# A graph network's count matrices on one core: layer-norm statistics ahead of all tiles, early turnings inside row 0, later rows placed in halves

## The reference, cut to what matters

```python
h = relu(layernorm(x))
# L0: three edge convolutions, all on the same edges
#   s[n] = sum over edges e with dst[e]=n of  concat(h[n], h[src[e]] - h[n]) @ W_l + b_l
#   h_l  = relu(s / max(cnt, 1));   cat = [h, h_1, h_2, h_3];   x1 = x + cat @ Wf + bf
# L1: one weighted convolution
#   agg[n] = sum over edges of edge_weight[e] * (relu(layernorm(x1)) @ W)[src[e]]
#   out = x1 + relu(batchnorm(agg + bias))
```

## Time and profile before

| | |
|---|---|
| median of 3 runs | 120.38 us |
| the three runs | 120.27, 120.38, 121.62 us |
| the profiled execution's own time | 121.34 us |
| its span (first to last instruction) | 118.6 us |
| mean granted TensorE clock | 0.992 |
| PE busy | 105.4 us (89%) |
| DVE busy | 96.0 us (81%) |
| ACT busy | 61.3 us (52%) |
| POOL busy | 26.9 us (23%) |

### The profile page before, as it was taken

One profiled execution on the slowest core, in us unless ns is written; L12 is line 12 of the kernel. 1 busy time (PEld: TensorE's weight loads), 2 busy tenths in 40 slices (PEclk: granted clock), 3 DMA queues, 4 the chain that ended last, 5 costly groups with the idle time before them and its releaser, 6 DMA issues.

```text
span 118.6 us, 2664 instructions
## 1 busy us (share of the span) xinstructions
PE 105.4 (89%) x1023; PEld 97.8 (82%) x1023; DVE 96.0 (81%) x269; ACT 61.3 (52%) x143; POOL 26.9 (23%) x32
## 2 busy tenths in 40 slices
PE   0298999999999999999989999999899998999740
PEld 0146889898799998998889999999899988998530
DVE  2499999999997999599997489965999979607970
ACT  2597765999679999330270613531613153223530
POOL 7100000000000069926039650099100000000000
PEclk9999999999999999999999999999999999999996
DMA  2967700000030000000050200000000000000025
GB/s 45 238 177 204 247 21 0 0 0 6 3 88 6 0 6 6 3 8 0 0 177 14 80 0 0 0 6 0 0 0 6 0 0 0 3 0 0 0 63 153
DMA packets 5400, 4.62 MB, mean 39 GB/s; under 512 B 555, under 2 KB 5386, under 8 KB 5386
## 3 DMA queue, kind: packets, MB, share of 16 engines
q1 hardware_dynamic: 4460, 3.68, 10.5%
q10 hardware_dynamic: 926, 0.75, 2.5%
HBM read 3.79 MB, written 0.64 MB: 37 GB/s over the span
## 4 chain that ended last, share of the span: by engine, by line
PE 60%; DVE 22%; POOL 6%; issue 4%; DMA 3%; ACT 3%; SPq 0%; DVEq 0%; POOLq 0%
PE bank L1217 11%; PE bank L1068 9%; PE bank L1312 9%; PE bank L1070 9%; PE bank L1069 9%; DVE src_hot L568 5%; PE bank L1130 4%; PE bank L1141 4%; DMA edge_rows_i<-in_dst_dram 3%; POOL parts L462 3%; POOL parts L464 2%; DVE stats L518 2%; PE bank L1108 2%; PE bank L1352 2%; DVE pre L732 2%
## 5 line engine op out<-in xcount | busy, mean ns | idle before, releaser
L1217 PEld LDWEIGHTS bank<-dst_hot,src_hot 125*128 125x128 bf16 x505 | 25.6, 104 | 3.5 <-DVE src_hot L568 1.8
L1217 PE MATMUL bank<-dst_hot,src_hot 125*128 125x112 bf16 (+6 forms) x505 | 27.7, 215 | 0.8 <-DVE src_hot L568 0.2
L568 DVE TENSOR_SCALAR src_hot<-node_id,edge_cols 125x626 bf16<-125x626 f16 x77 | 24.1, 380 | 0.6 <-PE bank L1217 0.6
L462 POOL TENSOR_TENSOR parts<-parts 125x625 f32<-125x625 f32 x5 | 7.0, 1391 | 46.4 <-DVE raw L575 39.2
L1312 PE MATMUL bank<-counts,u_lo 125*128 125x312 f32 (+1 forms) x60 | 16.3, 308 | 0.0
L1012 ACT ACTIVATE h_hi<-pre 128x312 fp32r<-128x312 f32 (+1 forms) x12 | 5.6, 468 | 18.0 <-DVE pre L732 18.0
L1312 PE MATMUL bank<-counts,u_hi 125*128 125x312 f32 (+1 forms) x48 | 14.0, 307 | 0.0
L879 ACT ACTIVATE parts<-bank 125x375 f32<-125x375 f32 x25 | 13.0, 536 | 0.0
L1312 PEld LDWEIGHTS bank<-counts,u_lo 125*128 125x128 f32 x60 | 10.9, 189 | 0.0
L1312 PEld LDWEIGHTS bank<-counts,u_hi 125*128 125x128 f32 x48 | 9.1, 189 | 0.0
L879 ACT ACTIVATE counts<-bank 125x125 fp32r<-125x125 f32 (+1 forms) x25 | 7.9, 317 | 1.1 <-PE bank L1217 1.1
(11 more groups left out here) (137 smaller groups left out, 258.6 us busy)
## 6 DMA issues: line engine op xcount, KB each, us to landing
raw<-in_L_gnn_W_dram SPq DMA_DIRECT2D x3, 512.0 KB, 6.8
x_in<-in_x_dram ACTq DMA_DIRECT2D x1, 560.0 KB
raw<-in_L_gnn_Wf_dram SPq DMA_DIRECT2D x1, 512.0 KB, 3.8
wf<-in_L_gnn_Wf_dram SPq DMA_DIRECT2D x1, 256.0 KB, 7.9
raw<-in_L_gnn_Wf_dram SPq DMA_DIRECT2D x1, 256.0 KB, 2.7
raw<-in_L_gnn_W_dram SPq DMA_DIRECT2D x1, 256.0 KB, 4.8
out_dram<-x_in SPq DMA_DIRECT2D x1, 224.0 KB
out_dram<-x_in SPq DMA_DIRECT2D x1, 168.0 KB
```

The lines of the kernel that those rows point to most:

```text
L462: step.add(pool.tensor_tensor(part[:, :, 1, :], part[:, :, 1, :], part[:, :, 2, :], ALU.add))
L568: dve.tensor_scalar(src_hot[:, t % RING, 0:IDS], node_id[:, 0:IDS], edge_cols[:, 0, t:t + 1], None, ALU.is_equal).then_inc(src_hot_vector, 1)
L1217: return pe.matmul(built[s][:, :, n0:n0 + n], src_hot[:, t % RING, BLK * s:BLK * s + P], dst_hot[:, c, :, j // 2, c0:c0 + n, j % 2], start ...
```

## The change: what it does

The statistics of x are all taken at once, ahead of the first weighted window, and the scale and shift right behind that window, before DVE's first tile. ACT makes tiles 0 and 4 early, then root, h0 and its copies, then tiles 22 and 27 with the high half of u's blocks 0 and 1 between them, and only then row 0's copies. PE runs ten matmuls without use instead of four, turns h0's blocks ahead of row 0's pieces 2, 4, 6, 9 and 9, the vectors ahead of piece 5, and makes u's blocks 0 and 1 ahead of piece 8. The banks of all these groups are named: the vectors have bank 6, and h0's block 3 is the next group in it. DVE reads the vectors at t = 18, u's low halves at t = 24, 37, 41. Rows 3 and 4 are placed in two halves as well.

```diff
-SCALAR_EARLY, SCALAR_LATER = (0, 4, 9), {0: (36, 40), 1: (55,), 2: (72, 76)}
-SCALAR_TILES = SCALAR_EARLY + sum(SCALAR_LATER.values(), ())
-STATS_AT, SHIFT_AT, VECS_AT, DIFF_AT = (1, 2, 3, 5, 6), 8, 19, 37
-U_AT = (34, 39, 42)
-DEV_AT, FLAG_AT = 40, 74
+SCALAR_EARLY, SCALAR_NEXT, SCALAR_LATER = (0, 4), (22, 27), {0: (36, 40), 1: (55,), 2: (72, 76)}
+SCALAR_TILES = SCALAR_EARLY + SCALAR_NEXT + sum(SCALAR_LATER.values(), ())
+VECS_AT, DIFF_AT = 18, 33
+U_AT = (24, 37, 41)
+DEV_AT, FLAG_AT = 43, 74
@@ the banks
-        groups.plan([("h0", b) for b in range(2)], h0_t_ready, 1)
-        groups.plan(["vecs"], vecs_ready, 1)
-        groups.plan([("h0", b) for b in range(2, NB)], h0_t_ready, 3)
-        for blocks in U0_BLOCKS:
-            groups.plan([("u", 0, blocks[0])], u_lo_ready, blocks[-1] + 1)
-        groups.plan([("own", 0, q) for q in range(4)], own_ready, 1)
-        groups.plan(["dev"], flag_ready, 1)
+        groups.plan([("h0", b) for b in range(2)], h0_t_ready, 1, banks=(7, 5))
+        groups.plan(["vecs"], vecs_ready, 1, banks=(6,))
+        groups.plan([("h0", 2)], h0_t_ready, 3, banks=(7,))
+        groups.plan([("u", 0, 0)], u_lo_ready, 2, banks=(5,))
+        groups.plan([("h0", b) for b in range(3, NB)], h0_t_ready, 4, banks=(6, 7))
+        groups.plan([("u", 0, 2)], u_lo_ready, 4, banks=(6,))
+        groups.plan([("u", 0, 4)], u_lo_ready, 5, banks=(7,))
+        groups.plan([("own", 0, q) for q in range(4)], own_ready, 1, banks=(5, 6, 7, 5))
+        groups.plan(["dev"], flag_ready, 1, banks=(6,))
@@ DVE
+            dve.wait_ge(x_loaded, 32)
+            for b in range(NB):
+                moments_of(b)
+            variances(range(NB))
             weighted_window(0)
+            scale_shift(range(NB), norm_ready)
             dve.wait_ge(edge_cols_ready, 1)
             for t in range(TILES):
-                if t in STATS_AT:
-                    dve.wait_ge(x_loaded, 32)
-                    moments_of(STATS_AT.index(t))
-                if t == STATS_AT[-1] + 1:
-                    variances(range(NB))
-                if t == SHIFT_AT:
-                    scale_shift(range(NB), norm_ready)
                 if t == VECS_AT:
@@ ACT
-            for t in SCALAR_EARLY[:3]:
+            for t in SCALAR_EARLY:
                 source_tile(t)
...
             root(rstd[0:BLK, 0:NB], moments[0:BLK, 0:NB, 1])
-            for t in SCALAR_EARLY[3:]:
-                source_tile(t)
...
             h0_high(NB - 1)
+            for t in SCALAR_NEXT:
+                source_tile(t)
+                if t == SCALAR_NEXT[0]:
+                    high_rows(("u", 0, 0), 0, 2)
...
                     copy_block(r, s)
-                    if r == 0 and s in (1, 3, 4):
-                        blocks = U0_BLOCKS[s // 2]
-                        high_rows(("u", 0, blocks[0]), blocks[0], len(blocks))
+                    if r == 0 and s == 2:
+                        high_rows(("u", 0, 2), 2, 2)
+                    if r == 0 and s == 4:
+                        high_rows(("u", 0, 4), 4)
@@ PE
-            keep_warm(4)
+            keep_warm(10)
...
-            jobs = {9: (0,), 11: (1,), 12: (2,), 14: (3,), 15: (4,)}
+            jobs = {2: (0,), 4: (1,), 6: (2,), 9: (3, 4)}
...
-                chunks = ((0, n // 2), (n // 2, n)) if r in (1, 2) else ((0, n),)
+                chunks = ((0, n // 2), (n // 2, n))
...
-                        if i == 12:
+                        if i == 5:
                             turn_vecs()
+                        if i == 8:
+                            neighbour_terms_0(U0_BLOCKS[:1])
                         for b in jobs.get(i, ()):
                             turn_h0(b)
...
-                            if r == NB - 1 and s == NB - 1:
+                            if r == NB - 1 and s == NB - 1 and chunk[0] == 0:
                                 sum_counts(1, fill(("cnt", 1))).then_inc(filled, 1)
...
                 if r == 0:
-                    neighbour_terms_0()
+                    neighbour_terms_0(U0_BLOCKS[1:])
```

More of the change, by code:

```diff
@@ L1120, in feature_rows, with neighbour_terms_0 @@
                 return [(hi[:, k, BLK * b:BLK * (b + 1)], lo[:, k, BLK * b:BLK * (b + 1)]) for k in range(KF)]
-            def neighbour_terms_0():
+            def neighbour_terms_0(groups_of_blocks):
                 pe.wait_ge(raw_loaded[0], 16)
-                for blocks in U0_BLOCKS:
+                for blocks in groups_of_blocks:
                     o = fill(("u", 0, blocks[0]))
```

## The result

The changed kernel takes 123.7 us (median of four, 123.6 to 124.62) against 120.57 (120.27 to 121.62): ratio 1.0306, 95% interval 1.025 to 1.0363. That is 3.1 us slower, where 0.8 was forecast, and above the top of the range, 122.7. The span of the profiled execution grew from 118.6 to 121.8 us.

The account below looks back on a forecast made before the run. The end was taken to hang on when DVE finishes tile 84: +1.73 wait for u, -0.29 for a tile, -0.64 wait at tile 68 gave +0.80 us, 121.2 us carried to the median; range 119.4 to 122.7.

Parts of the forecast that it names:

- The named banks cost nothing else.: Bank plan: u's banks 6 and 7 and own's banks are free in time, so no further cost.
- the last of the signs of being wrong: Layer 1, near 60 us: the forecast is wrong if PE and not DVE's head chain releases it.
- rival 2: PE's row 0: the clock stays low through it, by turnings or the new gap; +3.0 us, 123.4 us, chance 0.08.
- The vectors' wait: PE in front of piece 9 of row 0: a new wait of about 1.0 us, until 16.4, for DVE's copy.
- DVE's wait for u: DVE at t = 24: waits 1.73 us, 17.86 to 19.6, for the high half of u from ACT.
- DVE's finish: DVE's end of tile 84, at difference(1): 41.94 + 1.73 - 0.29 - 0.64 = 42.74, +0.80 us.
- The statistics: DVE ahead of all tiles: moving the five statistics nets 0, bounds 0 and +0.86 us for x landing late.
- The clock: PE's start: ten useless matmuls bring the upper clock level at 11.4 us instead of 17.6.
- the rule that the prediction takes from the Trainium skill: PE's clock: transposes don't count as activity, so turnings among row 0's first pieces would hold the clock down.
- The case against the rule: Kernel before, PE's row 0: five turned pairs stood in the 5.2 us before the clock's rise.
- Rows 3 and 4 in halves: PE's rows 3 and 4: the same 200 matmuls in halves, cost 0, bounds -0.3 and +0.5 us.
- That only DVE's waits reach the end: Up to about 42 us: DVE's waits cost in full; an earlier PE gives back at most 0.64 us.

Follow-up runs that it names:

- e1: The changed kernel with dev in bank 5 instead of bank 6, nothing else; 121.66 us, ratio 1.0109 to the kernel before.
- e2: The kernel before with dev alone put into bank 6 instead of bank 5; 122.26 us, ratio 1.013.
- e3: The changed kernel with 14 matmuls without use filling PE's wait for the flag ahead of the first count sums; 122.36 us, ratio 1.0187.
- e12: The changed kernel, dev still in bank 6, with DVE raising the flag at t = 64 instead of 74; 122.09 us, ratio 1.0167.
- e5: e1 with DVE copying the vectors at t = 10 instead of 18; 119.87 us, ratio 0.9986.
- e6: e5 with DVE taking u's first low halves at t = 28 instead of 24; 119.35 us, ratio 0.9877.
- e4: e1 with rows 3 and 4 placed whole, as before the change; 121.14 us, ratio 1.0064.
- e9: e6 with rows 3 and 4 placed whole, as before the change; 119.69 us, ratio 0.9967.
- e11: e1 with u's first low halves taken at t = 34 instead of 24, vectors still at t = 18; 120.37 us, ratio 1.0025.
- e8: The kernel before with difference(1) at t = 60 on DVE instead of behind t = 84; 125.51 us, ratio 1.0393.

## Why the prediction was wrong, point by point

- **Failed step: "The named banks cost nothing else."** The prediction went through the new groups of u and own, and not through `dev`, whose bank changed from 5 to 6 in the same lines. The wait moved to PE, 3.03 us, behind it the low clock, 1.4 us (e1, e2, e3, e12). Because of it PE, and not DVE, held the z step and layer 1, which is the last of the signs of being wrong that the prediction names. A low clock did cost time, but at row 3, behind a gap, and not in row 0, where rival 2 had it: that rival 2's 123.4 lies near the measured 123.7 is chance.
- **The vectors' wait**: forecast 15.4 to 16.4, measured 1.25 us up to 16.44. Right.
- **DVE's wait for u**: forecast 1.73, measured 1.68. Right. e5 shows that it hangs on the vectors' wait, and that the rest of the loss goes with the two; e6 takes away the last 0.3 us.
- **DVE's finish**: forecast +0.80 us, measured +0.69 (41.86 to 42.55). The statistics cost nothing, as forecast: DVE stood 0.23 us for x, but its first tile starts at 10.13 (forecast 10.16). Without the bank error the forecast (ratio 1.007, from 0.8 on 121.3) lies within e1's interval, 1.0058 to 1.016, and layer 1 starts 0.81 us later there.
- **The clock**: forecast up by 11.4. The last of the ten matmuls, which ends at 10.06, took 0.38 us and not 0.63, and the first pair of turnings spans 0.43 at 10.90. Right in kind, but the rise came at least 1.3 us sooner. Turnings stood among the first pieces; they ran at the upper level themselves, and the matmuls kept it. By the rule that the prediction takes from the Trainium skill (TensorE: Matmul & The Clock Gate, Part 4: PE-mode transpose) they would have held it down; this trace doesn't show that. The case against the rule is weaker than the prediction says: four pairs, not five, stood before the rise in the kernel before (the one at 17.60 already spans 0.42), with 35 matmuls of row 0 among them. Whether turnings alone would raise the clock no run shows.
- **Rows 3 and 4 in halves**: taken at 0, nothing found (e4, e9). ACT did wait 3.2 us for row 3's first block in the changed kernel, but PE's sums began right behind row 4.
- **That only DVE's waits reach the end** holds with dev in bank 5, and breaks in e11, where PE's 1.15 us come back through tile 68 and the sums. The rows show how narrow the margin was: PE waits only 0.40 us for `add_head` in the kernel before, so PE's own work ends little before DVE's, and the prediction put no price on a later PE.

## What to carry to other kernels

When a change names banks or buffers by hand, write out for each one the group before it, who reads that group and when, for every group in the changed lines, also for those that seem only to be carried along. A release that is early in one order is late in another. And an idle stretch on PE can cost twice: here about 1 us for the standing and 1.4 for the low clock behind it.

## What the runs showed of the hardware

- A gap of 1.25 us on PE left the clock up (50 matmuls in about 2.2 us behind it). Gaps of 2.10 us (e2) and 3.03 us were each followed by a granted clock of 0.50, until about 43.2 and 43.7 us. The fall doesn't stand in the gap: in the changed kernel PE resumes at 39.85 and the clock reads 1.00 up to 40.2 and 0.50 from 40.5 on; in e2 PE resumes at 38.28 and it reads 1.00 up to 39.6 and 0.50 from 39.9 on. In e8 it read 0.50 from 40 to 46 us, and there the gaps were of 0.57, 1.15 and 1.38 us with one or two matmuls between.
- The granted-clock row reads 1.00 in the first 18 us of the kernel before, although its matmuls there run at the 1.2 GHz level. The same instruction of 512 columns takes 0.63 us early in the changed kernel and 0.38 in e3's gap, both beside a reading of 1.00, so durations are the better witness (changed kernel, then e3; min, median and max in ns):

```profile
L1083 PE MATMUL bank<-node_id,zeros_bf x10: 380/634/634, 6.0 to 9.7; 125*128 125x512 f16 x10
L1263 PE MATMUL bank<-node_id,zeros_bf x14: 376/379/379, 36.7 to 39.5; 125*128 125x512 f16 x14
```

- A DVE source tile (bf16 out of f16) takes 0.38 us alone and 1.08 in the mean beside POOL's sums of 1.3 us each (e8). Not every DVE instruction pays: a reciprocal of 128 x 250 takes 1.72 us beside the sums in the kernel before (at 42.89) and 1.72 without them in e8, while the low half of a weight (`wb_lo`, L631) takes 1.33 beside them and 0.63 in e8.
- x lands at a moment that differs from execution to execution: with the statistics first, DVE didn't wait for it at all in e1 (start at 7.07) and e5 (7.39), and waited 0.23 us in the changed kernel (6.94), 0.47 in e6 (6.91), 0.72 in e9 (7.36) and 0.74 in e12 (7.13).
